# TensorE's loop of a long attention, walked in pairs of steps

## The reference

```
q = (query @ Wq + bq).reshape(B, Nq, H, D).transpose(0, 2, 1, 3)
k = (key_value @ Wk + bk)...
v = (key_value @ Wv + bv)...
attn = jnp.einsum('bhqd,bhkd->bhqk', q, k) * scale
attn = jnp.clip(attn, -CLAMP, CLAMP)
attn = jax.nn.softmax(attn, axis=-1)
attn = jnp.where(jnp.any(jnp.isnan(attn)), jnp.asarray(1.0 / Nkv, attn.dtype), attn)
x = jnp.einsum('bhqk,bhkd->bqhd', attn, v).reshape(B, Nq, Cq)
return x @ Wo + bo
```

## Time and profile before

| | |
|---|---|
| median of 3 runs | 363.79 us |
| the profiled execution | 366.83 us, its span 365.0 us |
| TensorE busy | 290.8 us (80%) |
| VectorE busy | 258.6 us (71%) |
| ScalarE busy | 175.3 us (48%) |
| GpSimd busy | 41.5 us (11%) |
| mean granted TensorE clock | 0.917 |
| the long attention's loop | 232.7 to 323.3 us of the span |

### The profile page before, as it was taken

How to read it: one execution, slowest core, us unless ns; L and a number is a source line. 1 busy time by engine, 2 the same in 40 slices (tenths; PEclk the granted TensorE clock), 3 DMA queues, 4 the chain that set the end, 5 groups by cost and what they waited for, 6 DMA issues and landing times.

```text
span 365.0 us, 7786 instructions
## 1 busy us (share of the span) xinstructions
PE 290.8 (80%) x3041; PEld 178.1 (49%) x3041; DVE 258.6 (71%) x671; ACT 175.3 (48%) x316; POOL 41.5 (11%) x97
## 2 busy tenths in 40 slices
PE   1039483979897997799999995678999999967954
PEld 1014321436363876744445552364666666643742
DVE  4799898967779956559334344975788888675735
ACT  3769595964737655130010000646667776711430
POOL 3042241700000210200020002300000000002002
PEclk9999786999999999699999996986999999995975
DMA  6980000000006997860000000000000000000000
GB/s 185 255 338 1 0 2 0 1 2 3 0 4 128 211 233 180 276 227 11 0 0 0 2 0 0 0 1 3 4 4 4 4 5 4 4 2 0 3 4 29
DMA packets 6320, 19.41 MB, mean 53 GB/s; under 512 B 1156, under 2 KB 2692, under 8 KB 5252
## 3 DMA queue, kind: packets, MB, share of 16 engines
q1 hardware_dynamic: 6277, 18.82, 18.7%
HBM read 12.07 MB, written 0.26 MB: 34 GB/s over the span
## 4 chain that ended last, share of the span: by engine, by line
PE 58%; DVE 29%; ACT 5%; DMA 4%; issue 2%; SPq 1%; POOL 0%; DVEq 0%; ACTq 0%
PE PS L1071 55%; DVE sm L684 5%; DMA cx<-ctx_in 4%; DVE yq L691 3%; DVE big L744 3%; PE PS L1260 2%; DVE w L847 2%; DVE sm L846 1%; DVE yq L753 1%; DVE yq L935 1%; ACT sa L373 1%; PE PS L1084 1%; SPq L254 1%; ACT xT L481 1%; DVE tern L932 1%
## 5 line engine op out<-in xcount | busy, mean ns | idle before, releaser
L1006 DVE TENSOR_REDUCE sm<-PS 128x1 f32<-128x512 f32 x64 | 43.3, 685 | 13.4 <-PE PS L1071 11.0
L307 POOL TENSOR_TENSOR rstd<-veps,mhalf 128x1 f32<-128x1 f32 x24 | 12.6, 548 | 213.7 <-DVE veps L572 213.7
L537 ACT ACTIVATE yq<-PS,sm 128x512 f32<-128x512 f32 x44 | 30.1, 687 | 13.9 <-PE PS L1071 13.6
L373 ACT ACTIVATE big<-PS,cols,sm 128x512 f32<-128x512 f32 (+1 forms) x40 | 32.3, 871 | 1.0 <-PE PS L1071 0.7
L1071 PE MATMUL PS<-sa,w 128*32 128x36 f32 (+1 forms) x320 | 30.8, 280 | 2.4 <-ACT w L504 2.4
L1071 PE MATMUL PS<-diag,ones 128*128 128x128 f32 x14 | 4.6, 424 | 35.0 <-DVE diag L617 25.0
L1071 PE MATMUL PS<-yq 128*128 128x384 f32 x96 | 31.1, 486 | 0.0
L1071 PE MATMUL PS<-big,yq 96*128 96x512 f16 x64 | 25.7, 407 | 4.6 <-DVE sm L1006 2.0
L1071 PE MATMUL PS<-yq,big 99*128 99x128 f16 x256 | 26.1, 225 | 2.8 <-ACT yq L541 1.5
L481 ACT COPY xT<-PS 128x512 f32<-128x512 f32 x5 | 2.9, 588 | 51.2 <-PE PS L1260 51.2
L1071 PEld LDWEIGHTS PS<-yq,big 99*128 99x128 f16 x256 | 19.4, 100 | 11.8 <-issue 6.6
(11 more groups left out here) (241 smaller groups left out, 602.2 us busy)
## 6 DMA issues: line engine op xcount, KB each, us to landing
big<-yq SPq DMA_DIRECT2D x24, 256.0 KB, 5.3
cx<-ctx_in SPq DMA_DIRECT2D x8, 384.0 KB, 10.7
w<-w_in SPq DMA_DIRECT2D x9, 256.0 KB, 5.0
yq<-w_in SPq DMA_DIRECT2D x1, 2304.0 KB, 10.5
wa<-wa_in SPq DMA_DIRECT2D x1, 1156.0 KB, 17.9
sa<-wx_in SPq DMA_DIRECT2D x1, 768.0 KB, 14.0
rows<-rows_in SPq DMA_DIRECT2D x1, 580.0 KB, 15.6
tern<-rows_in SPq DMA_DIRECT2D x1, 512.0 KB, 8.6
```

Of the source, the lines that this page charges most:

```text
L307: pool.tensor_tensor(rstd[:, t:t + 1], veps[:, t:t + 1], mhalf[:, t:t + 1], ALU.pow)\
L373: return nc.scalar.activation(o, i, func, bias=bias, scale=scale, **kw)
L537: nc.scalar.activation(pt(i), PS[:, ST_BANK[i % 2], :], ACT.Exp, scale=s1(M_ES))\
L1006: V.tensor_reduce(s1(M_MX + i % 8), PS[:, S_BANK[i % 3], :], AX, ALU.max, negate=True)\
```

## The change

TensorE's loop goes over two steps at a time. In a pair (n, n + 1) it does the two score products, then the rows of the maxima if they are due (n % 4 is 2), then the two groups of transposed scores, then the early value groups of the pair, then the outputs of index n - 14 and n - 13 (`LAG_O` goes from 13 to 14). VectorE's folding of the outputs begins one step later (at the third step of a batch instead of the second) and ends one step later. Nothing is added or removed in arithmetic, and no wait on a semaphore is added or removed. ScalarE's and GpSimd's instruction lists stay as they are.

```diff
-        LAG_T, LAG_O, ROWS_AT = 8, 13, 2
+        LAG_T, LAG_O, ROWS_AT = 8, 14, 2
@@ VectorE
-                    if b % 2 and b >= 5 and r >= 1:
-                        sum_heads((b - 5) // 2, r - 1)
-                        if r == 1:
+                    if b % 2 and b >= 5 and r >= 2:
+                        sum_heads((b - 5) // 2, r - 2)
+                        if r == 2:
                             sum_denominators((b - 5) // 2)
-                    elif b % 2 == 0 and b >= 6 and r < 3:
-                        sum_heads((b - 6) // 2, 3 + r)
+                    elif b % 2 == 0 and b >= 6:
+                        sum_heads((b - 6) // 2, 2 + r)
...
-            for n in (3, 4, 5):
+            for n in (2, 3, 4, 5):
                 sum_heads(B // 2 - 2, n)
@@ TensorE
-            for n in range(R * B + LAG_O):
+            for n in range(0, R * B + LAG_O, 2):
                 b, r = n // R, n % R
-                if n < R * B:
-                    scores(n)
-                if 0 <= n - LAG_T < R * B:
-                    transposed_scores(n - LAG_T)
-                if (b, r) in VALUE_STEPS:
-                    context_values(2, VALUE_STEPS.index((b, r)))
-                if n >= LAG_O:
-                    outputs((n - LAG_O) // 4, (n - LAG_O) % 4)
+                for i in (n, n + 1):
+                    if i < R * B:
+                        scores(i)
                 if r == ROWS_AT and 1 <= b <= B:
                     maxima_rows(b - 1)
+                for i in (n - LAG_T, n + 1 - LAG_T):
+                    if 0 <= i < R * B:
+                        transposed_scores(i)
+                for i in (n, n + 1):
+                    if (b, i % R) in VALUE_STEPS:
+                        context_values(2, VALUE_STEPS.index((b, i % R)))
+                for i in (n - LAG_O, n + 1 - LAG_O):
+                    if i >= 0:
+                        outputs(i // 4, i % 4)
```

## The result

The changed kernel takes **377.28 us** (median of 4 runs, 376.91 to 377.57), the kernel before in the same comparison 365.75 (4 runs, 363.44 to 368.34). The ratio is 1.038, with a 95% interval of 1.035 to 1.042: slower. It is larger than the quotient of the two medians (1.032) because it leaves out runs in a slower state that some executions show, here those of the kernel before at 367.71 and 368.34 us. The forecast was 368.8 with a range of 362.5 to 373.0. Its direction was right, its size was not: the profiled execution went from 366.83 to 376.91, so by +10.1 where the working had +5.0.

A forecast was written before the change was run, and what follows sets the result against it. TensorE was taken to set the pace. Middle +4.2, start 0 and end +0.8 gave +5.0 on the profiled 366.83, so 371.8, less 3.0 to the median: 368.8 us, range 362.5 to 373.

The forecast's parts named there:

- Changes of width: TensorE, between products of 128 and 32 weight columns: 0.23 us there and back; fewer changes bring a batch from 4.71 to 4.44.
- The first rival: TensorE's wait shrinks and only the saved changes count: 3.5 us gained, 360 to 361; 0.20 including half the wait.
- The wait for the exponentials: TensorE's second transposed group waits 0.63 us a batch for ScalarE; batch 5.07 instead of 4.71, +4.2 us in the middle.
- T + 2.85: Earliest start of the next pair's second transposed group; T starts a rows pair's first group; without waits T + 2.22.
- Start: Loop start: a value group falls behind the fourth score product, +1.05 or more, caught up later; +0, bounds -1 and +2.
- End: Last two batches, without score products: paired batch 4.50 instead of 4.37; +0.8 us, bounds 0 and +1.5.
- From the profile to the median: Last step of the sum: 371.8 for the profiled execution, which stood 3.0 above the median, so 368.8 us.
- The clock in the middle: Rival: TensorE's new idle time lowers the clock for 15 of 60 us, 6 us more, 375; chance 0.15.
- VectorE: Rival: two maxima and the folding meet, score products wait, some 0.2 a batch more, 371 to 372; chance 0.05.
- The forecast's own bounds: Whole kernel: bounds of loop start and last batches, -1.8 to +2.7 around 368.8, given as 366 to 372.5.

The follow-up runs named there:

- the rows between: Kernel before the change, unpaired, with the rows of the maxima moved between score product and transposed group in their step: 369.33 us, ratio 1.019.
- the last kernel: Changed kernel with LAG_T 10, rows behind outputs, copy behind both exponentials, value groups at their old place, one pair of If blocks: 357.59 us, ratio 0.981.
- The experiment on the value groups: Changed kernel with the five early value groups back behind their own score products: 375.71 us, ratio 1.028.

## Why the prediction was wrong

**Changes of width: right.** 0.23 per pair of changes came back as 4.94 with the rows between, and as 2.00 and 2.22 per pair in the last kernel. "Tiling Modes" in the Trainium skill's "TensorEngine Tiling (Array Packing)" says that a change of mode drains TensorE; the traces agree in that a change costs time, 0.23 us there and back, and can't show that this is a drain. The first rival priced this gain rightly. It needed the chain gone, and other edits than this change do that.

**The wait for the exponentials: right in place and kind, its size was the failed step.** I had T + 2.85 for the second group and 0.63 of waiting. Measured from 272.03 to 275.14 it is 3.11. By links: first exponentials +0.44 (I took 0.42), copy +0.71 (0.60, my estimate between 0.57 and 0.69; it is the upper bound), second exponentials +0.60 (0.61), their duration 0.69, to the product 0.67 (0.53). The last link is the sequencer: in its own records the first compare-and-branch behind the wait takes 0.33 in some batches of the middle and 0.42 in others, where it took 0.21 in the row I read the earlier trace rows. Six of the ten batches from 261.45 on take 5.29 to 5.30; the four with 0.42 take 5.37 to 5.42. I had one sample of this link, from the loop's start, and gave it no bound, although the trace of the kernel before had a longer one of this branch (shortest, median and longest in ns):
```profile
L1403 PEldq COMPARE_BRANCH  x64: 207/213/345, 245.2 to 319.8; - x64
```
In sum 4.44 + 0.15 at the first group + 0.72 at the second = 5.31 a batch, 0.24 above my 5.07. With the longer batches the middle is +6.75 instead of +4.2.

One link was missing altogether. Even with its exponentials in time, the second group can stand up to 0.92 behind the first, since its wait is reached only some 0.3 behind the first group's start (experiment with the copy first). In the changed kernel the exponentials end at about that point (274.47, where the first group's start plus 0.3 is 274.50), and the distance is 0.94 against 0.82 to 0.92 where the sequencer alone set it. By this reading faster exponentials alone would have brought little; no run tests just that.

**Start: +1.4 instead of 0.** I named the value group behind the fourth score product (+1.05 to 2.1) and then cancelled it against idle time of 244 to 249 us. Less was caught up than I took: the first transposed group waits for the copy behind everything else, so a delay before it goes through, and it comes 2.14 later (9.20 against 7.06 behind the fourth score product). Of this 0.8 is made up by the fifth batch, which leaves +1.35. The experiment on the value groups gives back 2.15, a part of which may be the clock. The result lies within my bound of +2, but I had put the value at 0.

**End: +2.1 instead of +0.8.** Without score products the chain meets less cover. TensorE in the last batches of the changed kernel:
```profile
322.21 0.39 PE L1071 MATMUL PS<-yq,big 99*128 99x128 f16 x4 [0.53 <-ACT yq L541]
323.03 0.46 PE L1071 MATMUL PS<-yq,big 99*128 99x128 f16 x4 [0.43 <-issue]
```
Two waits in one pair, 0.53 for the copy and 0.43 behind it, and the same again at 326.82 and 327.64. I had the batch at 4.50; from 322.21 to 326.82 it is 4.61. The rest of the miss lies at the entry and at the last groups, which I did not take apart.

**From the profile to the median: wrong.** I took off 3.0, since the profiled execution of before stood 3.0 above its median. The changed kernel has no such distance (376.91 in the profile, 377.28 in the median). The kernel before scatters from 361.5 to 369.2 in all its runs here, and its time goes with its granted clock: 0.930 to 0.939 at 361.5 to 362.1, 0.912 to 0.917 at 367 and above. The changed kernel stands at 0.910 in all four. The one profile of each shows where a difference in half clock lies between these two executions. In 235.6 to 259.5 us the kernel before is at half clock for 10 us:
```profile
235.60:249.30 13.70, 9.83 (x67) 7.19 (x65) 10.27 (x23) 7.62 (x12) 0.85 (x1) 0.88 0.01 2
249.30:259.50 10.20, 9.56 (x125) 5.98 (x129) 5.72 (x16) 5.62 (x10) 0.00 (x0) 0.67 0.01 2
```
and the changed one, by its rows above, for 17. The last step of the sum should have stayed inside one kind of number, with the spread in the range.

**The rivals.** The clock in the middle: refuted, 1.00 from 259.5 to 333.4 us although 10% of the middle is idle. The Trainium skill's "TensorE: Matmul & The Clock Gate", section "A second HAM failure mode: psum-queue depth-cycling", tells of a kernel whose clock goes back and forth with short idle times; with gaps of 0.5 to 0.7 in a batch of 5.3 the trace shows nothing of it. At the start of the loop, with idle times of up to 2.85 us (238.38), the granted clock does fall (0.75 and 0.50 in the rows above). VectorE: refuted, since at a batch of 4.24 TensorE is busy for all of 44.00 us and VectorE is not.

**Forecast in order.** +4.2, 0, +0.8 and -3.0 against +6.75, +1.35, +2.11 and none. The three in the loop are 5.2 us and the translation 3.0; with 0.4 by which this median stands above its profile, less 0.1 outside the loop, they are the miss of 8.5 (377.28 against 368.8). So the step that weighed most inside the loop is the wait, taken at 0.63 a batch and measured at 0.87 (0.15 and 0.72); the translation to the median weighed as much. The forecast's own bounds hold a slip besides: -1.8 from 368.8 is 367.0, not 366.

## What to carry to other kernels

When two groups that use alternating buffers are moved next to each other, count the time from release to reuse again for the second one, with all that the releasing engine does in between. Put a wait inside the branch, or ahead of work that hides it: from the end of the exponentials to the product 0.05 us passed inside the block here, 0.14 in straight code, and 0.53 to 0.80 with two `If` blocks behind the wait. A gain per batch (0.47 to 0.49 us of 4.71 here) arrived only once the waits were off the path, so move the dependence first and the order second.

## What the hardware showed that I had not expected

- A copy behind exponentials on ScalarE starts only at their recorded end (0.71 behind their start, they take 0.69), while exponentials behind exponentials start 0.58 apart and exponentials behind a copy 0.60.
- With the same two branches between 0.53 and 0.80 pass from the end of the exponentials to the product (274.47 to 275.14 is 0.67). What sets the first one's 0.21, 0.33 or 0.42 no run here shows.
- One unchanged kernel has more half clock in some executions than in others: the kernel before ran at 361.5 to 362.1 us with a mean clock of 0.930 to 0.939, and at 367 and above with 0.912 to 0.917. Where in its faster executions the half clock lies, no profile here shows.
